# A state-space block and eight experts in one sweep over the batches: four batches in flight instead of three, and key sums formed as rows-by-features products

## The chip, the cores and the metric

The kernel runs on one core of a Trainium2 chip. The metric is device time in microseconds (us) of that core, as the median of three runs. TensorE (PE) multiplies matrices into PSUM, which has eight banks of 128x512 float32 here; VectorE (DVE), ScalarE (ACT) and GpSimd (POOL) work beside it, and SyncE (SP) issues most transfers. Each engine takes its instructions strictly in the order in which the program lists them. They meet through semaphores.

## The reference

Two layers of a modulated ("adaLN") network over x of 16 batches x 512 tokens x 128 features:

```
h = layernorm(x)*(1+ca)+sa
# layer 0, mixer: a selective state-space scan over the tokens, 256 channels, 16 states
xb, zb = split(h @ in_proj); xb = silu(conv4(xb)); zb = silu(zb)
dt, B, C = split(xb @ x_proj); dt = softplus(dt @ dt_proj + dt_bias)
for each of 16 states n:  s_n = exp(dt*A_n)*s_n(previous token) + dt*B_n*xb ;  y += C_n*s_n
x = x + ga * ((y + xb*D) * zb) @ out_proj
# layer 0, feed-forward: every expert computed, the best of 8 kept per token
h = layernorm(x)*(1+cb)+sb ;  x = x + gb * gate * (relu(h @ w1[e] + b1[e]) @ w2[e] + b2[e])
# layer 1, attention with random features (16 heads of 64), then ELU feed-forward and two norms
h3 = modulated layernorm(x)
k = h3@Wk ; v = h3@Wv ; kf = exp(k@proj - |k|^2/2 - M) + eps      # M: largest over ALL batches
kv = kf^T v ; ksum = sum over tokens of kf
out = (qf @ kv) / (qf @ ksum) @ Wo ...
# layer 1, feed-forward: 16 experts, two kept per token, plus a shared one
```

Since M is a maximum over all batches, the keys' sums of every batch must be formed before the queries of any batch can use them: the kernel has two sweeps.

## The kernel before, in words

**First sweep** (layer 0 and the key sums of layer 1). One step of the loop serves three batches: `a` runs its sixteen states, `b` (the one before) its experts and, in the same step, its keys, and `n` (the next) its norm, projections and convolution. A fourth name, `y`, only finishes key sums of the batch before `b`. 18 steps run: one with `n` alone, 16 with a state batch `a`, and one with `b` alone. Steps 3 to 14 are a hardware loop.

A step is cut by hand into slots. In each slot VectorE does for one state k, in this order: the input `u` (L1031), the scan `h` (L1038, `tensor_tensor_scan`), the weighing `zz` (L1047). Other work is listed between them. TensorE spreads B_k and C_k of each state over 128 partitions (`spread`, L801), which `u` and `zz` wait for. ScalarE makes the decay exponentials of the next state (`decay`, L591, two of them), which wait for the scan of this slot, since their buffer is double. GpSimd adds `zz` to the sum (L728).

Around this, in slots 2 to 11, lie the experts: 32 `ups` (each three 128x512 products in split precision, L174 to L176, by `split_product`), which go through a ring of three PSUM banks (2, 3, 4) that ScalarE's `relu` (L616) empties; eight `downs` (L854, 16 products of 128x128 each, banks 5 and 6), each taken by VectorE in the next slot (L1100). In slots 12 to 16 come the norm for layer 1 (L3), and eight key tiles (`key_tile`): each has three 128x512 products k, d, v (L869), a ScalarE square of k (L638) and a copy of v (L641), and on VectorE a reduction, a maximum and the exponent (L1125, L1128, L1131). At the end of the step: the largest key, softplus, the output projection (L809), the first residual, and the key exponentials (L648). The products `kf^T v` with a column of ones beside v (`key_sums`, L892) are 32 products of 128x129 in banks 5, 6 and 7. ScalarE copies them out (L655) and issues their store (L659).

The projections of `n` and `a` (x, z) and the logits share bank 7. Those of the step size dt and of B, C use banks 0 and 1.

**Second sweep.** Step by step, batch `n` loads its key sums, `c` computes queries, and `d` is in the feed-forwards. The C ring has two banks (0 and 1). At the end of a step the engines do this:

```
if n is not None:            # TensorE
    value_sums(n)            # two products, ring entries vs0, vs1
if d is not None:
    down(NX - 2, d); down(NX - 1, d)
...
if d is not None:            # VectorE
    dve.wait_ge(*mo(d, 1)); ... fo = ffn * gab
if n is not None:
    keys(n)                  # builds kvb for the next step's queries (L1821, L1823)
```

and the next step begins on TensorE with `query(0, "q")` (L174 to L176), which waits for its bank: the ring entry two before it must be done. Before, these entries were `vs0` and `vs1`, done when ScalarE had copied them (`evs_ok`, L1455).

## Time and profile before

| | us |
|---|---|
| median of three runs (range) | 3930.2 (3924.9 to 3931.4) |
| the profiled execution, its own time | 3920.3 |
| its span, first to last instruction | 3918.5 |
| PE busy / share | 3002.6 / 77% |
| DVE busy / share | 2898.4 / 74% |
| ACT busy / share | 1855.8 / 47% |
| POOL busy / share | 861.6 / 22% |
| mean granted TensorE clock, share of full | 0.889 |

The first sweep ends at about 2403 us, the second has its first VectorE work at 2421.7 us and takes the rest. A busy share is an average over both. A row of the timeline gives the start, how long it lasted (merged pieces with their count), engine, line, operation, output and input, and in brackets how long the engine had been idle and what released it. Tile names lose their numbers: `kvs` is `sq` for the key squares, `dt`, `dec`, `h`, `zz` are those above. A float32 product appears as two MATMUL records.

### The profile page before, as it was taken

The page shows a single profiled execution, that of the slowest core. Times are in us where ns is not written, and L with a number is a line of the kernel's source. Part 1 is how long each engine was busy: PE and PEld are TensorE (multiplying, and loading weights), DVE is VectorE, ACT ScalarE, POOL GpSimd, SP SyncE. Part 2 cuts the span into 40 slices and gives each one's busy share as a digit, 9 for nine tenths or more (in the row PEclk, how much of TensorE's full clock was granted, in tenths as well). Part 3 has the DMA queues.
Part 4 walks back from the last instruction along what each step waited for, and adds up shares of the span by engine and source line. Part 5 has one row for each costly group of instructions (what it writes and reads, how often), then busy time and mean ns, then how long its engine had stood idle before and what let it go on. Part 6 is the DMA issues. An engine that isn't in the chain of part 4 may idle for free. (4 is left out here: it accounts for less than half of the span.)

```text
span 3918.5 us, 51287 instructions
## 1 busy us (share of the span) xinstructions
PE 3002.6 (77%) x16104; PEld 2238.1 (57%) x16104; DVE 2898.4 (74%) x4942; ACT 1855.8 (47%) x2856; POOL 861.6 (22%) x590
## 2 busy tenths in 40 slices
PE   2478678777877867867877785788887888888886
PEld 1156446546545645645644663666666666666665
DVE  4888888888888888888888844666666666666664
ACT  3456546646645645645654642433333333333332
POOL 0433332333233323233323310011111111111111
PEclk6589889889988988988988897999999999999998
DMA  2000000000000000000000001000000000000000
GB/s 98 4 11 8 18 12 12 12 11 12 12 12 16 7 17 11 7 17 11 7 17 8 13 9 62 21 16 15 15 15 21 15 15 15 15 15 15 23 7 10
DMA packets 49767, 64.28 MB, mean 16 GB/s; under 512 B 3584, under 2 KB 36416, under 8 KB 49184
## 3 DMA queue, kind: packets, MB, share of 16 engines
q1 hardware_dynamic: 47392, 54.93, 4.3%
q10 hardware_dynamic: 2304, 8.46, 0.5%
q8 instruction: 37, 0.61, 0.1%
q14 instruction: 34, 0.28, 0.0%
HBM read 41.78 MB, written 21.60 MB: 16 GB/s over the span
## 5 line engine op out<-in xcount | busy, mean ns | idle before, releaser
L728 POOL TENSOR_TENSOR acc<-acc,zz 128x1024 f32<-128x1024 f32 x256 | 605.6, 2365 | 1400.4 <-DVE h L1038 1376.6
L1038 DVE TENSOR_TENSOR_SCAN h<-dec,u 128x1024 f32<-128x1024 f32 x256 | 584.4, 2283 | 3.5
L591 ACT ACTIVATE dec<-dt,aneg 128x512 f32<-128x512 f32 (+1 forms) x512 | 340.2, 712 | 439.1 <-DVE h L1038 415.2
L801 PE MATMUL bank<-S,pick_sb 96*128 96x512 bf16 x512 | 218.8, 439 | 386.1 <-DVE zz L1047 321.9
L854 PEld LDWEIGHTS bank<-one_sb,hid 128*128 128x128 f32 x4096 | 477.4, 192 | 4.6
L854 PE MATMUL bank<-one_sb,hid 128*128 128x128 f32 x4096 | 478.6, 274 | 0.0
L801 PEld LDWEIGHTS bank<-S,pick_sb 96*128 96x128 bf16 x512 | 52.6, 105 | 548.6 <-DVE zz L1047 375.7
L158 POOL TENSOR_SCALAR n_ve<-n_mv 128x4 f32<-128x4 f32 x96 | 33.5, 349 | 1344.3 <-DVE n_mv L141 1344.3
L1047 DVE TENSOR_TENSOR zz<-h,bank 128x1024 f32<-128x1024 f32 x256 | 312.5, 1221 | 8.8
L1031 DVE TENSOR_TENSOR u<-dtx,bank 128x1024 f32<-128x1024 f32 x256 | 311.0, 1215 | 9.9 <-DVE dtx L1024 7.4
L1446 ACT ACTIVATE uq<-uq 128x512 f32<-128x512 f32 x128 | 80.8, 631 | 359.9 <-DVE uq L1809 359.9
L616 ACT ACTIVATE hid<-banks,one_sb 128x512 f32<-128x512 f32 x336 | 227.5, 687 | 49.7 <-PE banks L176 48.1
L1508 ACT ACTIVATE th<-bank 128x512 f32<-128x512 f32 x160 | 95.6, 597 | 304.7 <-PE bank L176 303.7
L1100 DVE COPY_PREDICATED facc<-oh,bank 128x512 f32<-128x512 uint32 x128 | 93.0, 727 | 183.9 <-PE bank L854 183.5
L174 PE MATMUL bank<-h4h,low 128*128 128x512 f32 x192 | 102.2, 532 | 94.7 <-DVE sl L1893 69.9
L174 PE MATMUL banks<-hT2h,w_low 128*128 128x512 f32 x336 | 151.1, 450 | 21.3 <-ACT hid L616 21.3
L1711 PE MATMUL bank<-two_sb,hm 128*128 128x128 f32 x1280 | 158.9, 277 | 2.3 <-DVE hm L1899 2.3
L1711 PEld LDWEIGHTS bank<-two_sb,hm 128*128 128x128 f32 x1280 | 153.1, 193 | 10.6 <-issue 6.7
L1642 PEld LDWEIGHTS bank<-two_sb,aT 128*128 128x128 f32 x1024 | 142.0, 201 | 16.0 <-ACT aT L1467 4.0
L1626 PE MATMUL banks<-kvb,qT 128*128 128x130 f32 x1024 | 144.5, 286 | 5.6 <-DVE at L1835 5.6
L1899 DVE SCALAR_TENSOR_TENSOR hm<-sl,bank 128x512 f32<-128x512 f32 x160 | 109.9, 687 | 49.7 <-PE bank L1702 44.6
L1642 PE MATMUL bank<-two_sb,aT 128*128 128x128 f32 x1024 | 142.1, 284 | 3.0 <-ACT aT L1467 3.0
(256 smaller groups left out, 6897.5 us busy)
## 6 DMA issues: line engine op xcount, KB each, us to landing
kv_dram<-kvs ACTq DMA_DIRECT2D x16, 516.5 KB, 3.1
kvl<-kv_dram SPq DMA_DIRECT2D x16, 516.5 KB, 3.5
xs<-in_x SPq DMA_DIRECT2D x16, 256.0 KB, 2.8
x<-in_x SPq DMA_DIRECT2D x16, 256.0 KB, 2.8
x_dram<-x SPq DMA_DIRECT2D x16, 256.0 KB, 2.1
h_dram<-hT SPq DMA_DIRECT2D x16, 256.0 KB, 2.0
h<-h_dram SPq DMA_DIRECT2D x16, 256.0 KB, 2.6
x2s<-x_dram SPq DMA_DIRECT2D x16, 256.0 KB, 2.7
```

The source lines that it names most:

```text
L174: pe.matmul(dst, lhs[1], rhs[0], start=True, stop=False)
L591: act.activation(dec[:, k % 2, g, g:], dt[:, g, g:], ACT.Exp, scale=aneg[:, g, k:k + 1]).then_inc(dec_ok.sem, 1)
L616: act.activation(hid[:, e % 2, f, :], bank1(f"up{n}"), ACT.Relu, bias=b1c[:, n:n + 1]).then_inc(hid_ok.sem, 1)
L728: pool.tensor_tensor(acc[:, :, :], acc[:, :, :], zz[:, k % 2, :, :], ALU.add)\
L801: pe.matmul(banks[which][:, :], pick_sb[:, at:at + 1].to_broadcast([96, P]), S[0:96, :], start=True, stop=True).then_inc((cbc if which els ...
L854: last = pe.matmul(bank1(f"down{e}")[:, j * D:(j + 1) * D], hid[:, e % 2, f, j * P:(j + 1) * P], w2[:, e, f, :], start=(f == 0), stop=(f = ...
L1031: dve.tensor_tensor(u[:, :, :], dtx[:, :, :], mid(banks[0][:, :], G), ALU.mult)\
L1038: dve.tensor_tensor_scan(h[:, :, :].rearrange("p g t -> p (g t)"), dec[:, k % 2, :, :].rearrange("p g t -> p (g t)"), u[:, :, :].rearrange ...
L1047: dve.tensor_tensor(zz[:, k % 2, :, :], h[:, :, :], mid(banks[1][:, :], G), ALU.mult)\
L1626: last = pe.matmul(pair[:, k // 2, at_k:at_k + 2 * HW], qT[:, m % 2, k * P:(k + 1) * P], kvb[:, 4 * s + k, :], start=True, stop=True)
L1642: last = pe.matmul(banks[4][:, j * D:(j + 1) * D], aT[:, m % 2, k * P:(k + 1) * P], wo[:, 4 * s + k, :], start=False, stop=(s == 1 and k = ...
L1711: last = pe.matmul(banks[7][:, j * D:(j + 1) * D], hm[:, q, j * P:(j + 1) * P], w, start=(q == 0 and j == 0), stop=(q == NX - 1), skip_gro ...
```

## The change

**First sweep, four roles.** A step now serves `y` (two before the state batch: its norm L3 and its keys), `b` (one before: gated output, first residual, experts), `a` (states) and `n`. There are 19 steps: one with `n` alone, 16 with `a`, one with `b` and `y`, one with `y` alone. Slots run 0 to 16. All tables of slots are new, and a bank's next use now waits for the last use by a list of names and roles (`freed`, `free1`).

**Places.** z's projections go into the ring of three banks beside the ups; x, B/C/dt and logits have bank 7 to themselves, so banks 0 and 1 hold the spreads alone. ScalarE's `decay` stands first in its slot, before the relus. The positive part of dt moves from VectorE (`positive`, L1016, two of 128x512) to ScalarE (`magnitude`, one more activation each). B and C are split in a second tile `Sn` and copied to `S` by ScalarE (`keep_split`).

**Key sums.** No v and no copy of v. Instead h3 is turned back to rows (`back3`, `keep_rows`), and `products` forms h3^T kf as eight products of 128x512 (four for each half). `sums` forms the sums over tokens by eight 32x512 products with ones, four of them into the four quarters of one bank. `turn_sums` adds the quarters and turns them to columns by eight 128x128 products. In the second sweep `key_values` multiplies the loaded h3^T kf by Wv: eight products of 128x128 in two new ring entries kv0, kv1, which are free when VectorE's `keys` is done (`kvb_ok`).

```diff
-            UPS = {2: (0, 1), 3: (2, 3), 4: (4, 5), 5: (6, 7), 6: (8, 9), 7: (10, 11), 8: (12, 13), 9: (14, 15)}
-            DOWNS = {3: 0, 4: 1, 5: 2, 6: 3, 7: 4, 8: 5, 9: 6, 10: 7}
-            KEYS = {13: (0, 1), 14: (2, 3), 15: (4, 5), 16: (6, 7)}
-            GATE = {4: 0, 5: 1}
+            KEYS_PRE = {5: (5,), 6: (7,)}
+            KEYS_POST = {2: (0, 1), 3: (2, 3), 4: (4,), 5: (6,)}
+            TILE_A = {3: 1, 4: 2, 5: 4, 6: 6}
+            TILE_Z = {2: 0, 4: 3, 5: 5, 6: 7}
+            UPS_PRE = {4: (2,), 7: (8,), 8: (11, 12), 9: (16,), 10: (18,), 11: (20,), 12: (23,), 13: (25,),
+                       14: (27,), 15: (29,)}
+            UPS_POST = {3: (0, 1), 4: (3,), 5: (4, 5), 6: (6, 7), 7: (9, 10), 8: (13, 14, 15), 9: (17,), 10: (19,),
+                        11: (21, 22), 12: (24,), 13: (26,), 14: (28,), 15: (30, 31)}
+            DOWNS = {6: 0, 7: 1, 9: 2, 10: 3, 12: 4, 13: 5, 15: 6, 16: 7}
+            EXPS = {7: 0, 8: 1, 9: 2, 10: 3}
+            XIN = {9: 0, 10: 1}
+            CONV = {10: 0, 11: 1}
+            ring = ["oproj", "turn3", "k0", "back3", "turn2", "k1", "k2", "up0", "up1", "k3", "up2", "k4", "up3",
+                    "k5", "k6", "up4", "up5", "z0", "z1", "k7", "up6", "up7"]
...
+                    def step(s):
+                        y, b, a, n = roles(s)
+                        for slot in range(SLOTS):
                             if a is not None and slot + 1 <= NS - 1:
                                 decay(slot + 1, a)
...
+                            if a is not None and slot == 6:
+                                silu_z(0, a)
+                                silu_z(1, a)
...
+                            if y is not None:
+                                for m in KEYS_PRE.get(slot, ()):
+                                    key_square(m, y)
+                            if b is not None:
+                                for q in UPS_PRE.get(slot, ()):
+                                    relu(q, b)
...
+                        if n is not None:
+                            keep_split(a, n)
                             decay(0, n)
+                        if y is not None:
+                            store_sums(y)
...
-                    def key_sums(j, a, b, n):
+                    def products(half_k, y, s):
+                        pe.wait_ge(*h3n_ok(y, 1))
+                        free1(pe, f"g{half_k}", s)
+                        for j in range(J):
+                            pe.wait_ge(*kf(y, j + 1))
+                            last = pe.matmul(bank1(f"g{half_k}"), h3n[:, j, :], Ek[:, j, half_k * T:(half_k + 1) * T],
+                                             start=(j == 0), stop=(j == J - 1))
+                        last.then_inc(gps.sem, 1)
+
+                    def sums(half_k, y, s):
+                        free1(pe, f"ks{half_k}", s)
+                        for j in range(J):
+                            last = pe.matmul(bank1(f"ks{half_k}")[32 * j:32 * j + 32, :], ones[:, 0:32],
+                                             Ek[:, j, half_k * T:(half_k + 1) * T], start=True, stop=True)
+                        last.then_inc(ksps.sem, 1)
...
-        ringC = [("vs0", evs_ok, 1), ("vs1", evs_ok, 2)]
+        ringC = [("vs0", evs_ok, 1), ("vs1", evs_ok, 2), ("kv0", kvb_ok, 1), ("kv1", kvb_ok, 1)]
...
+                def key_values(c):
+                    pe.wait_ge(*kv_in(c, 16))
+                    for s in range(2):
+                        freeC(pe, f"kv{s}", c)
+                        for r in range(PR // 2):
+                            pr = s * (PR // 2) + r
+                            last = pe.matmul(bankC(f"kv{s}")[:, r * P:(r + 1) * P], kvl[:, pr * P:(pr + 1) * P],
+                                             wv[:, pr * P:(pr + 1) * P], start=True, stop=True)
+                        last.then_inc(kvps.sem, 1)
...
                     if n is not None:
                         value_sums(n)
+                        key_values(n)
                     if d is not None:
                         down(NX - 2, d)
```

ScalarE, first sweep, the looped step. Before, two gate activations (zs) lie in two slots, the relus (hid) between them, and the spare rows are the waits:

```order
L591 ACTIVATE dec<-dt,aneg 128x512
L591 ACTIVATE dec<-dt,aneg 128x511
L552 ISA
L554 ACT_TABLE_LOAD
L554 ACTIVATE zs<-bank 128x512
L614 REGISTER_ALU
L615 REGISTER_ALU
L616 ACTIVATE hid<-banks,one_sb 128x512
```

Now, in slot 6 (Gs is the tile of the key squares, here that of tile 7):

```order
L621 ACTIVATE dec<-dt,aneg 128x512
L621 ACTIVATE dec<-dt,aneg 128x511
L573 ISA
L575 ACT_TABLE_LOAD
L575 ACTIVATE zs<-bank 128x512
L573 REGISTER_ALU
L575 ACTIVATE zs<-banks 128x512
L671 REGISTER_ALU
L675 ACTIVATE Gs<-banks 128x512
```

The square of key tile 7 and the relus of ups 6 and 7 (the rows that follow) now stand behind the decays, a table load and both gates.

TensorE, first sweep, slot 15 to the end of the looped step as it is now (L921 is a down, L966 the new sums, L869 the spreads, L976 the turn of the sums):

```order
L921 MATMUL bank<-one_sb,hid 128x128 x16
L497 REGISTER_ALU
L966 MATMUL bank<-Ek,ones 32x512 x4
L869 MATMUL bank<-S,pick_sb 128x512
L917 REGISTER_ALU
L497 REGISTER_ALU
L921 MATMUL bank<-one_sb,hid 128x128 x16
L966 MATMUL bank<-Ek,ones 32x512 x4
L865 REGISTER_ALU
L869 MATMUL bank<-S,pick_sb 128x512 x2
L976 MATMUL bank<-thirty,kss 128x128 x8
```

Before, this place held the largest key, the output projection, the spreads and half of the key sums; the downs were over by slot 10. Now two downs and the sums stand in it, and the last spread of C is behind the first sums.

TensorE, second sweep, the border of the looped step. Before:

```order
L1601 MATMUL bank<-keep_sb,hsB 128x512 x2
L1711 MATMUL bank<-two_sb,hm 128x128 x4
L1709 REGISTER_ALU
L1711 MATMUL bank<-two_sb,hm 128x128 x4
L1381 REGISTER_ALU
L1381 COMPARE_AND_BRANCH
```

Now:

```order
L1686 MATMUL bank<-keep_sb,hsB 128x512 x2
L1691 ISA
L1432 ISA
L1696 MATMUL bank<-keep_sb,kvl 128x128 x4
L1432 REGISTER_ALU
L1696 MATMUL bank<-keep_sb,kvl 128x128 x4
L1807 MATMUL bank<-two_sb,hm 128x128 x4
L1805 REGISTER_ALU
L1807 MATMUL bank<-two_sb,hm 128x128 x4
L1466 REGISTER_ALU
L1466 COMPARE_AND_BRANCH
```

Eight products came in ahead of the last two downs (L1807), and the query products that open the next step follow the branch as before.

## Rows read from the trace of the kernel before

**Rows 1.** Busy time in one looped step of the first sweep (windows)
```profile
core 0: us, PE busy (x) PEld busy (x) DVE busy (x) ACT busy (x) POOL busy (x), PEclk, DMA share, GB/s
1026.80:1169.76 142.96, 111.22 (x554) 78.24 (x553) 120.42 (x161) 80.14 (x116) 43.74 (x25) 0.88 0.04 12
```

**Rows 2.** Line L1024, once at the end of each step (source view)
```profile
L1024 DVE TENSOR_TENSOR dtx<-dt,xc x16: 1224/1225/1226, 78.8 to 2166.1; 128x1024 f32<-128x1024 f32 x16
```

**Rows 3.** VectorE's waits in the step of rows 1: total, times, longest
```profile
DVE facc L1100 <- PE bank L854: 9.2, 5, 2.4
...
DVE ssq L1125 <- ACT kvs L638: 2.5, 2, 1.9
...
DVE xh L149 <- POOL n_rs L160: 1.5, 1, 1.5
...
DVE idx L1079 <- DVE m L1075: 0.2, 1, 0.2
```

**Rows 4.** VectorE's timeline, first sweep
```profile
177.95 1.23 DVE L1024 TENSOR_TENSOR dtx<-dt,xc 128x1024 f32<-128x1024 f32 x1
...
1117.06 2.29 DVE L1038 TENSOR_TENSOR_SCAN h<-dec,u 128x1024 f32<-128x1024 f32 x1
...
1121.86 2.29 DVE L1038 TENSOR_TENSOR_SCAN h<-dec,u 128x1024 f32<-128x1024 f32 x1
...
1141.40 0.68 DVE L1125 TENSOR_REDUCE ssq<-kvs 128x8 f32<-128x512 f32 x1
...
1143.32 2.28 DVE L1038 TENSOR_TENSOR_SCAN h<-dec,u 128x1024 f32<-128x1024 f32 x1
...
1161.74 1.40 DVE L1016 TENSOR_SCALAR dt<-bank,one_sb 128x512 f32<-128x512 f32 x2
```

**Rows 5.** ScalarE's timeline, first sweep
```profile
1061.82 0.69 ACT L616 ACTIVATE hid<-bank,one_sb 128x512 f32<-128x512 f32 x1
...
1112.21 1.33 ACT L591 ACTIVATE dec<-dt,aneg 128x512 f32<-128x512 f32 x2 [8.04 <-DVE h L1038]
1113.56 1.28 ACT L549 ACT_TABLE_LOAD   x1
...
1137.74 0.58 ACT L638 ACTIVATE kvs<-bank 128x512 f32<-128x512 f32 x1
...
1163.79 4.27 ACT L648 ACTIVATE Ek<-Ek,ncb 128x1024 f32<-128x1024 f32 x4
```

**Rows 6.** TensorE's timeline, first sweep
```profile
1054.88 3.73 PE L854 MATMUL bank<-one_sb,hid 128*128 128x128 f32 x32
...
1060.22 0.40 PE L174 MATMUL banks<-hT2h,w_low 128*128 128x512 f32 x1
...
1062.32 0.39 PE L801 MATMUL bank<-S,pick_sb 96*128 96x512 bf16 x1
...
1113.49 0.61 PE L801 MATMUL bank<-S,pick_sb 96*128 96x512 bf16 x1 [7.85 <-DVE zz L1047]
...
1141.77 1.02 PE L869 MATMUL bank<-one_sb,hT 128*128 128x512 f32 x2
```

**Rows 7.** VectorE at a border between steps of the second sweep (timeline)
```profile
2939.30 0.69 DVE L1952 TENSOR_TENSOR fo<-bank,gab 128x512 f32<-128x512 f32 x1 [1.25 <-PE bank L1711]
...
2942.78 0.69 DVE L1803 TENSOR_REDUCE qs<-qsqb 128x8 f32<-128x512 f32 x1
```

**Rows 8.** TensorE at the same border (timeline)
```profile
2935.44 1.91 PE L1601 MATMUL bank<-keep_sb,hsB 128*128 128x512 f32 x4
2937.18 2.08 PE L1711 MATMUL bank<-two_sb,hm 128*128 128x128 f32 x16
2939.02 0.48 PE L174 MATMUL bank<-high,h3l 128*128 128x512 f32 x1
```

**Rows 9.** The end of the first sweep: last take, and the last store's issue (timeline)
```profile
2358.28 0.72 DVE L1100 COPY_PREDICATED facc<-oh,bank 128x512 f32<-128x512 uint32 x1 [2.84 <-PE bank L854]
...
2402.99 0.34 ACTq L659 DMA_DIRECT2D kv_dram<-kvs  x1
```

More of the change, by code:

```diff
@@ new lines, in adaln_depth2 @@
+            DOWNS = {6: 0, 7: 1, 9: 2, 10: 3, 12: 4, 13: 5, 15: 6, 16: 7}
+            TAKES = {slot + 1: e for slot, e in DOWNS.items() if slot + 1 < SLOTS}
+            EXPS = {7: 0, 8: 1, 9: 2, 10: 3}
[3 more added lines that the diff above has]
+                    "k5", "k6", "up4", "up5", "z0", "z1", "k7", "up6", "up7"]
+            ring += [f"up{n}" for n in range(8, 25)] + ["gates", "up25", "up26", "b2"]
@@ new lines, in roles, with free1 @@
+            def roles(s):
+                return tuple(batch_at(s, off) for off in (YES, BEF, NOW, NXT))
+            def free1(pe, name, s):
+                names = uses[bank_of[name]]
+                at = names.index(name)
+                before = [(back, other) for back in range(3) for other in reversed(names[:at] if back == 0 else names)]
+                for back, other in before:
+                    off, done, count = freed[other]
+                    batch = batch_at(s, off - back)
+                    if batch is not None:
+                        pe.wait_ge(*done(batch, count))
+                        return
@@ L899, in step @@
-                    def step(a, b, n, y):
-                        for slot in range(END):
+                    def products(half_k, y, s):
[6 more added lines that the diff above has]
+                        last.then_inc(gps.sem, 1)
@@ L901, in step @@
+                    def step(s):
+                        y, b, a, n = roles(s)
+                        for slot in range(SLOTS):
                             k = slot - 1
```

828 lines of the change are left out of this document (427 added, 401 removed).

## The prediction, made before the changed kernel had run

> **What bounds the kernel now.** I read the page first, then windows of one step of each sweep, VectorE's waits in one step, and the timelines of single slots. One looped step of the first sweep takes 143 us; VectorE is busy for 120.4 of them, TensorE for 111.2, at a granted clock of 0.88 [rows 1]. From the first to the last L1024, once a step, are 2087.3 us; less the first interval of 99.2 there are fourteen of 142.0 [rows 2, 4]. So VectorE sets the step, and what can be saved is its idle time: twelve lines of waits, from 9.2 down to 0.2 us, sum to 20.4 us [rows 3]. Of these 9.2 are takes that wait for a down: ups and down of an expert are packed into each slot there. VectorE's own work with its gaps is then 143.0 - 20.4 = 122.6 us. A better order of the other engines can win at most the waits for them, some 19 us a step, and only if it makes no new ones.
>
> **The change, part by part.** *Removed from VectorE*: the positive part of dt, 1.4 us [rows 4]. With 0.7 us of short waits between its own instructions, which stay, its work is 122.6 - 1.4 + 0.7 = 121.9 us a step. A bare slot (scan to scan) is 4.8 us, a key tile 1.9 [rows 4].
>
> *TensorE's work* hardly changes. Gone are eight v products and 32 narrow ones. A 512-wide float32 product keeps it for 0.86 us (two records, 1.02 with the tail of the last); a down for 3.6; an up for 0.70 (2.10 us from the record at 1060.22 to the spread, nine records) [rows 6]. Eight v products were 6.9 us and the 32 narrow ones about 8. New are eight h3^T kf products, 6.9, the turn back, 0.6, the turn of the sums, 1.9, and the sums. For these no row is near: no product here fills a quarter of a bank. Bounds: four after one another 4 x 0.86 = 3.4 us, four at once 0.9. I take the middle, 2.1 for each half. TensorE's sum per step stays near 102 us.
>
> The Trainium skill, page "TensorE: Matmul & The Clock Gate", section "Part 3: Packing small matmuls", says that products whose outputs lie in different 32-partition strips run concurrently; no run here shows it yet. By it the sums would be near the 0.9 us; that is a rival below.
>
> *ScalarE* loses eight v copies (0.6 each), three sum copies and two of eight table loads, and gains two relus of dt, five copies and one more small one: about even, 80 us of 142 [rows 1]. But its place changes. In every slot it now first waits for that slot's scan, then makes two decays (1.3 us), and only then the relus (0.7) and squares (0.6) [rows 5] that TensorE's three-bank ring waits for. So each slot holds a loop: scan, decays, relus, ups, down, take. I walked through the slots with the rows' durations; S is the end of the slot's scan. VectorE's new waits:
> - slots 1 and 2: both norms wait for GpSimd, as before at 1.5 for one [rows 3]: 0.5 + 1.5. Key tile 0 waits for its square at S + 1.9 while zz ends at S + 1.2: 0.8.
> - slot 5, tile 5: the same, 0.8.
> - slot 6, tile 7: decays 1.3, table load 1.3, two gates 1.1, square 0.6: S + 4.3 against S + 1.2: **3.0**.
> - slot 7: ups 6 and 7 wait for the banks of z (S + 3.2), down 0 ends at S + 8.3, the largest key is spread at S + 9.0 to 10.5 (after six idle us TensorE is slow: 7.85 us of idling are followed by a spread of 0.61 instead of 0.39 [rows 6]). VectorE is there at S + 7.5: **2.2**.
> - slot 10: up 14 waits for the relu of up 11, S + 2.0; four ups, turn, spreads, down 2: S + 9.5. The bare slot 9 is over, so the take waits **2.6**, the convolution for x another 1.0; slot 11 1.4.
> - slot 13: decays, three relus, a copy, two table loads (one before, one after) and the silu, two relus, two copies end 11.3 after the scan of slot 11; VectorE is there at 8.7: **2.6**; slot 14 0.6.
> - slots 14 to 16 on TensorE: 1.3 to the bias product's end, 5.1 ups, products, dt, then 2.5 of ups, down, sums, down: take 6 waits 1.2, the last C 0.3, softplus 1.8 (its logarithm stands behind the copy of the first sums).
>
> Sum 20.3, so a step is 121.9 + 20.3 = **142.2 us**: the takes' waits are gone, but waits on ScalarE have come in their place.
>
> *Transfers and GpSimd.* SP now loads the residual x and both gate rows for `b` when x2 of the batch before is done, at a step's end. VectorE wants them after gated output, norm, scan, zz and projection, about 8 us later, and such loads land in 2.8 us (the page's list of transfers): nothing. The stores are the same size. GpSimd's L2 norm now stands before its first addition and L3's after its last; the additions have a slot of 7 us for 2.4 us of work, so only the two norm waits listed remain. The copy of B and C at the step's end waits for the last sums and ends before VectorE's second residual (3.1 us): hidden, but 1 to 2 us late if the sums take 3.4.
>
> *The sweep.* Start and first interval stay (78.8 + 99.2). The next step has no keys: 142.2 less eight tiles (15.4), one norm and the largest key (2) and their waits (5), 120. Then thirteen steps of 142.2. The last L1024 comes at 2146.6 instead of 2166.1: -19.5. From there to the end of the last take were 2359.0 - 2166.1 = 192.9 [rows 2, 9]. Now follow a step without n, 127 (142 less about 15 for n), and one for b and y that TensorE sets: eight downs 28.6, 32 ups 22.4, sixteen key products 13.8, h3^T kf 6.9, sums 2.1, rest 6, and 15 of opening chain, 95. That is 222: +29. The last batch's keys now stand alone, without v (-4 of the 44 us from the last take to the store's issue [rows 9]), but behind its exponentials (4.3 us for four [rows 5]) stand, instead of narrow products that ran along with them, four products (3.4), both sums (4.2), the turn (1.9) and copies: +7. The first sweep so ends 12 to 14 us later.
>
> *The border of the second sweep.* Before, value sums, two downs, then at once the first query (2939.02) [rows 8]; fo and the keys' assembly ran beside it until 2942.78, where the first reduction found its square ready [rows 7]. Now eight 128-wide products (16 records at 0.117, by the down of 3.73 for 32 [rows 6]) delay the last downs by 1.8 us, and the first query waits for `kvb_ok`, so for fo and the assembly; then come three records (0.9 with the tail) and the square (0.6) before the reduction. 1.8 + 1.5 = 3.3 us, 15 times: **+50**. The assembly itself, four half-size instructions for two, is even. Nothing covers it: every engine's next step starts from this border. If slack covered it, it would cost nothing.
>
> Sum: -19.5 + 29 + 3 + 50 = about **+64**. The profiled execution took 3920.3 us: 3984; it lay 10 us under the median of 3930, so I forecast **3990** for a median.
>
> **The rivals.**
> - *ScalarE's order hides after all*, 0.20. For: it is busy for only 80 of 143 us, and some waits of my list may overlap. Then slots 6, 7, 10 and 13 lose half of their 10 us: step near 137, 15 steps x 5.2 = -78: **3912**. It decides on the other side where the step falls under 138.2, since 15 x 4 = 60 pays for the rest.
> - *The sums at once*, 0.15: four quarter-bank products in the time of one, as the section named above has it. The sums then end 1.2 us earlier in each half: softplus waits 0.9, the last C nothing, so a step is 141.0 and the end 2 us shorter: **3970**. In the other direction, at 3.4 us each, 4010, which is in my forecast's own range.
> - *The second sweep's border is covered*, 0.08: the later query shortens waits that follow within the step: **3940**. Against: VectorE is in line from fo to the reduction without a gap [rows 7].
> - *The loop gets slower*, 0.17. TensorE's idle pieces of 3.5 to 6 us in slots 1, 5, 6 and 8 leave it at the lower level (1.2 GHz) while ups and downs are due, 2 to 3 us in two places: step 147, **4062**. Against: before, it idled as long (7.85 us [rows 6]) and met its takes.
> - The forecast itself, 0.40, its own range 3955 to 4030.
>
> **How the numbers follow.** A difference of 0.2% (8 us) is about what a measurement of this kernel can tell from none. Slower: 0.40 + 0.15 + 0.17 + 0.05 of the covered border = 0.77. Faster: 0.17 of the first rival and 0.01 = 0.18. The rest, 0.05, is within. The range 3900 to 4060 leaves out some 0.08 of the fast rival and 0.09 of the slow one.
>
> **What will show it.** In the new profile: L1024's successor thirteen times at 142 us apart; VectorE's wait for ScalarE's square of 3 us in slot 6 and for the copy of B and C of 2.6 in slot 13, while waits of takes for downs fall from 9.2 to about 4; the clock near 0.88; at the second sweep's border a TensorE idle of 3.5 us before the first query, released by VectorE's kvb, and 95.7 us a step for 92.4. If the distance of steps is under 138 us, my reading of ScalarE's order is wrong; if the border shows no such idle, the ring is.

## The result, and the profile after

The changed kernel takes 4122.3 us (median of 4 runs, 4116.4 to 4127.1) against 3927.5 for the kernel before in the same comparison (also 4 runs): ratio 1.049, 95% interval [1.047, 1.051]. The forecast was 3990. The sign is right, the size is not: +195 us instead of +64. The profiled executions differ by 199.8 us of span (4118.3 and 3918.5), divided by a few landmarks of the two timelines:

| stretch | before | after | difference | forecast |
|---|---|---|---|---|
| start to the last dtx (L1024, now L1097) | 2166.1 | 2249.6 | +83.5 | -19.5 |
| from there to the end of the last take | 192.9 | 222.8 | +29.9 | +29 |
| to the last store's issue | 44.0 | 48.0 | +4.0 | +3 |
| to the first VectorE work of sweep two | 18.7 | 18.4 | -0.3 | 0 |
| sweep two up to the first fo (two borders) | 151.7 | 160.2 | +8.5 | |
| its next 14 steps, fo to fo | 1276.0 | 1349.2 | +73.2 | +50 with the row above |
| the last step and the end | 69.1 | 70.1 | +1.0 | |

The end of the first sweep came out within 2 us. The looped step and the border of the second sweep did not. Busy time in a looped step, as [rows 1]:

```profile
core 0: us, PE busy (x) PEld busy (x) DVE busy (x) ACT busy (x) POOL busy (x), PEclk, DMA share, GB/s
1047.94:1198.31 150.37, 110.92 (x525) 75.23 (x525) 122.58 (x159) 73.42 (x113) 44.67 (x25) 0.89 0.04 12
```

150.4 us, not 142.2. VectorE is busy for 122.6 us although 1.4 us of work left it: [rows 1] had 120.4. Line L1097, as [rows 2]:

```profile
L1097 DVE TENSOR_TENSOR dtx<-dt,xc x16: 1225/3254/3261, 84.2 to 2249.6; 128x1024 f32<-128x1024 f32 x16
```

The same instruction took 1.22 us sixteen times before; now only the first does, and the median is 3.25. VectorE's waits in the step from 897.84 to 1047.94, as [rows 3]:

```profile
DVE facc L1177 <- PE bank L921: 5.6, 3, 3.2
DVE ssq L1203 <- ACT Gs L675: 4.3, 3, 3.0
DVE u L1103 <- issue: 4.0, 2, 3.7
DVE cb L1222 <- PE bank L949: 3.2, 1, 3.2
DVE cv L1066 <- ACT xpad L564: 3.0, 2, 1.9
DVE Sn L1079 <- ACT Sn L583: 2.1, 1, 2.1
DVE zz L1119 <- PE bank L869: 0.8, 1, 0.8
DVE dt L1094 <- ACT cv L608: 0.7, 1, 0.7
```

The walk through the slots is nearly all there: 3.0 for the square in slot 6, 3.2 (forecast 2.2) for the largest key, takes, copies of x, the split (2.1 for 2.6); the takes fell from 9.2 to 5.6. Not there are the waits of the two norms for GpSimd (2.0 forecast), and a wait of 0.8 at zz was not forecast. All waits, with the short ones that are not shown, sum to 25.4 us; 3.7 of them are the one line that was not forecast at all, "issue": a wait for nothing that the profile shows. Another 1.6 are short waits between VectorE's own instructions, for which the forecast had 0.7. What is left, 20.1 us, stands against the forecast's 20.3. Where the wait for issue is, VectorE's timeline over a border of steps shows:

```profile
1044.40 1.22 DVE L1119 TENSOR_TENSOR zz<-h,bank 128x1024 f32<-128x1024 f32 x1
1046.35 1.56 DVE L1094 TENSOR_TENSOR dt<-xpad,cv 128x1024 f32<-128x1024 f32 x1 [0.73 <-ACT cv L608]
1047.94 3.25 DVE L1097 TENSOR_TENSOR dtx<-dt,xc 128x1024 f32<-128x1024 f32 x1
...
1055.96 0.38 DVE L141 BATCH_NORM_AGGREGATE n_mv<-n_st 128x2 f32<-128x6 f32 x4 [0.16 <-DVE n_st L136]
1059.83 1.22 DVE L1103 TENSOR_TENSOR u<-dtx,bank 128x1024 f32<-128x1024 f32 x1 [3.50 <-issue]
```

GpSimd at the same time:

```profile
1044.45 5.67 POOL L794 TENSOR_TENSOR acc<-acc,zz 128x1024 f32<-128x1024 f32 x2 [4.65 <-DVE h L1110]
```

The loop's branch stands between n_mv and u. The wait of 3.4 to 4.1 us is there at the end of each of the loop's twelve turns but the first. The two full steps without it take 147.1 and 147.0 us, the others 150.0 to 150.4. The border of the second sweep, VectorE, as [rows 7]:

```profile
3181.32 0.69 DVE L2055 TENSOR_TENSOR fo<-bank,gab 128x512 f32<-128x512 f32 x1 [3.00 <-PE bank L1807]
3181.93 1.46 DVE L1918 TENSOR_SCALAR kvb<-kvl,sfac 64x8 f32<-64x8 f32 x2
3183.40 1.98 DVE L1926 SCALAR_TENSOR_TENSOR kvb<-bank,sfac,evs 64x256 f32<-64x256 f32 x4
3187.12 0.69 DVE L1900 TENSOR_REDUCE qs<-qsqb 128x8 f32<-128x512 f32 x1 [1.75 <-ACT qsqb L1527]
```

and TensorE, as [rows 8]:

```profile
3179.33 1.95 PE L1807 MATMUL bank<-two_sb,hm 128*128 128x128 f32 x16
3185.52 0.47 PE L174 MATMUL bank<-high,h3l 128*128 128x512 f32 x1 [4.24 <-DVE kvb L1926]
```

The idle time before the first query is there, released by kvb, 4.2 us for 3.5. From fo to the first reduction are now 5.8 us in this step and 6.5 in most others (before 3.5 [rows 7]), and 14 steps average 96.4 us for 91.1.

### The profile page after: what moved, and what is told of

It reads as the page before. It is cut to its first block and busy times, and to the rows that moved or that the text cites. A ratio compares the mean times of both kernels' runs of the same rounds, so it can differ in the third digit from the quotient of the medians.

```text
span 4118.3 us, 51446 instructions
## 1 busy us (share of the span) xinstructions
PE 3078.8 (75%) x15912; PEld 2234.9 (54%) x15912; DVE 2946.7 (72%) x4942; ACT 1752.8 (43%) x2792; POOL 872.4 (21%) x590
## 5 line engine op out<-in xcount | busy, mean ns | idle before, releaser
L794 POOL TENSOR_TENSOR acc<-acc,zz 128x1024 f32<-128x1024 f32 x256 | 618.4, 2416 | 1200.9 <-DVE h L1110 1193.1
L869 PE MATMUL bank<-S,pick_sb 96*128 96x512 bf16 x512 | 227.3, 449 | 379.4 <-DVE u L1103 224.2
L921 PEld LDWEIGHTS bank<-one_sb,hid 128*128 128x128 f32 x4096 | 498.8, 199 | 14.7 <-issue 2.2
L921 PE MATMUL bank<-one_sb,hid 128*128 128x128 f32 x4096 | 496.7, 281 | 0.9 <-DVE facc L1177 0.8
L158 POOL TENSOR_SCALAR n_ve<-n_mv 128x4 f32<-128x4 f32 x96 | 49.5, 516 | 1677.0 <-DVE n_mv L141 1677.0
L869 PEld LDWEIGHTS bank<-S,pick_sb 96*128 96x128 bf16 x512 | 53.3, 104 | 589.8 <-DVE u L1103 270.6
L174 PE MATMUL banks<-hT2h,w_low 128*128 128x512 f32 x336 | 210.3, 626 | 95.7 <-ACT hid L653 64.4
L943 PE MATMUL bank<-pk,hT 128*128 128x512 f32 x256 | 157.8, 703 | 9.4 <-DVE Ek L1210 7.9
L1900 DVE TENSOR_REDUCE qs<-qsqb 128x8 f32<-128x512 f32 x128 | 87.3, 682 | 102.9 <-ACT qsqb L1527 102.8
L1807 PE MATMUL bank<-two_sb,hm 128*128 128x128 f32 x1280 | 157.3, 276 | 2.3 <-DVE hm L2002 2.3
L174 PE MATMUL bank<-hT2h,w_low 128*128 128x512 f32 x176 | 100.1, 569 | 74.5 <-ACT zs L575 74.5
L174 PEld LDWEIGHTS banks<-hT2h,w_low 128*128 128x128 f32 x336 | 72.6, 216 | 149.6 <-ACT hid L653 85.9
L1807 PEld LDWEIGHTS bank<-two_sb,hm 128*128 128x128 f32 x1280 | 151.0, 193 | 3.3 <-DVE hm L2002 2.7
```

Of the source, the lines that this page charges most:

```text
L174: pe.matmul(dst, lhs[1], rhs[0], start=True, stop=False)
L794: pool.tensor_tensor(acc[:, :, :], acc[:, :, :], zz[:, k % 2, :, :], ALU.add)\
L869: pe.matmul(banks[which][:, :], pick_sb[:, at:at + 1].to_broadcast([96, P]), S[0:96, :], start=True, stop=True).then_inc((cbc if which els ...
L921: last = pe.matmul(bank1(f"down{e}")[:, j * D:(j + 1) * D], hid[:, e % 2, f, j * P:(j + 1) * P], w2[:, e, f, :], start=(f == 0), stop=(f = ...
L943: pe.matmul(bank1(f"{name}{m}"), hT3[:, j * P:(j + 1) * P], w[:, half_m * T:(half_m + 1) * T], start=True, stop=True).then_inc(done.sem, 1)
L1807: last = pe.matmul(banks[7][:, j * D:(j + 1) * D], hm[:, q, j * P:(j + 1) * P], w, start=(q == 0 and j == 0), stop=(q == NX - 1), skip_gro ...
```

## Experiments

Each ran beside the kernel before on its own chip; its median there was 3925 to 3929. Medians, and ratios to the kernel before:

| run | edit | us | ratio, 95% interval |
|---|---|---|---|
| e1 | changed, 50 idle instructions before the loop | 4094.4 | 1.042 [1.038, 1.045] |
| e2 | before, 79 idle instructions | 3949.5 | 1.005 [1.004, 1.007] |
| e3 | changed, keys ahead of fo | 4061.0 | 1.034 [1.030, 1.037] |
| e4 | changed, own banks for h3^T kf Wv | 4089.3 | 1.040 [1.036, 1.043] |
| e5 | changed, dt behind the residual | 4123.8 | 1.050 [1.048, 1.053] |
| e6 | changed, square 7 first | 4139.0 | 1.054 [1.051, 1.056] |
| e7 | e1, e3 and e5 together | 4024.9 | 1.024 [1.022, 1.027] |
| e8 | before, keys ahead of fo | 3922.2 | 0.998 [0.997, 0.9995] |
| e9 | changed, last addition cut (result incomplete) | 4096.3 | 1.043 [1.040, 1.046] |
| e10 | e7, down 0 later | 4028.1 | 1.026 [1.023, 1.029] |
| e11 | changed, sums in turn | 4166.2 | 1.059 [1.057, 1.061] |
| e12 | e7, gates ahead of the decays | 3933.7 | 1.001 [1.000, 1.002] |
| e14 | changed, gates ahead of the decays | 4043.0 | 1.029 [1.027, 1.031] |
| e13 | e12, convolution later | 3899.3 | 0.993 [0.991, 0.994] |
| e15 | e13, take 2 later | 3878.6 | 0.987 [0.985, 0.989] |

**The wait at the branch (e1, e2).** In the changed kernel's step five packets of 8 KB of instructions are fetched, at 907.9, 910.7, 920.5, 972.7 and 1034.9 us. The branch itself is at 906.0. From the program's order the last three fetches fall at instructions 32, 160 and 288 of VectorE's loop body of 333, so 128 apart (in the trace's records of VectorE, some of which are extra, at 38, 170 and 293 of 337). Its loop starts 49 instructions earlier than before and, if blocks are 128 long, lies over four of them.

```diff
                     dve.wait_ge(a_exp, 1)
+                    for _ in range(100):        # e1; e2, on the kernel before: range(158)
+                        dve.wait_ge(a_exp, 1)
```

> The changed kernel with 50 idle wait instructions (100 waits on a count reached long before, two to an instruction) ahead of the first sweep's loop on VectorE, nothing else. Fetch theory: the wait of 3.5 us before the first state input after the loop's branch is VectorE's loop body lying over four blocks of 128 instructions (the trace fetches 5 packets of 8 KB a step, at loop positions near 32, 160 and 288 of 333), with the branch's target thrown out by the last fetch. Shifted by 50 the body lies in three: instruction packets fall from 89 to about 34, the eleven waits of 3.4 to 4.1 us vanish, each looped step takes 147.1 us as the two unrolled ones do, not 150.2: 34 us less, about 4088. Rival: the wait belongs to what stands there (the semaphores, GpSimd, the end of the norm), then all stays within 8 us of 4122 and the row still shows 3.5 us.

> The kernel before with 79 idle wait instructions ahead of VectorE's first loop. Fetch theory: its body (314 instructions) begins 49 later than that of the changed kernel, so 79 more put it in the same position to the blocks of 128 and it now lies over four of them: instruction packets rise from 34 to about 90, a wait of 3 to 4 us with nothing that releases it appears at the branch of each of the last eleven looped steps (there was a wait of 0.6 there), 11 x 3 = +33 us, about 3960. Rival (position has no part in it): within 8 us of 3928.

The page's line of instruction packets, of the changed kernel, e1 and e2 (packets, MB, share):

```profile
q14 instruction: 89, 0.73, 0.1%
```

```profile
q14 instruction: 34, 0.28, 0.0%
```

```profile
q14 instruction: 90, 0.74, 0.1%
```

e1 has no wait for issue at the branch any more, and its looped steps take 146.6 to 147.0 us; e2 has eleven of 3.1 to 3.2 us, one of them this:

```profile
1042.30 1.22 DVE L1033 TENSOR_TENSOR u<-dtx,bank 128x1024 f32<-128x1024 f32 x1 [3.06 <-issue]
```

So the wait is made and taken away by instructions that do nothing: it hangs on the position of VectorE's loop body to the blocks in which instructions are fetched. The median gains 28 us here; the steps alone say 37 (11 x 3.4). In the kernel before e2 lost 22 us, less than the 33 expected. Only some 11 of them lie in the looped steps, which grew by 1.0 us (143.4 for 142.4): the wait for the logits fell there from 2.2 to 0.7 us and the wait of 0.6 behind dtx went. Another 7 lie at the start, where the first dtx comes at 86.1 us for 78.8, which fits an estimate of 0.09 us for each idle instruction (e1 starts some 4 us later, too).

In e1's profile the last dtx comes 36 us earlier, but the span is only 20 shorter: its second sweep was slower (97.4 us a step for 96.4), with no edit there. So a difference of 1 us a step of the second sweep between two profiles shows nothing.

The Trainium skill, page "Runtime: NRT & Kernel Launch", section "Instruction fetch mechanics", says that each engine has a small instruction memory refilled in blocks, and that a taken branch to a target outside the window forces a fetch before execution goes on. By that rule the prediction would have had to look at the branch. The trace agrees with it at the branch, but its fetches are of 8 KB, 128 instructions apart, where the page has blocks of 16 KiB.

**GpSimd's last additions (e5, e9).** e5 moves dt and dtx behind the last take and the second residual.

```diff
-                        norm_stats(dve, L3, x2, b, passed)      # the end of second_residual
...
-                        if n is not None:
-                            softplus(n)
                         if b is not None:
                             take(E0 - 1, b)
                             second_residual(b)
+                        if n is not None:
+                            softplus(n)
+                        if b is not None:
+                            norm_stats(dve, L3, x2, b, passed)
```

> The changed kernel with VectorE's last take and second residual (up to the sum x2) ahead of dt and dtx at the step's end, and the norm's statistics behind them; GpSimd's last two additions are then over before dt begins. Theory (the two additions on GpSimd slow VectorE's instructions whose operands all lie in SBUF): dtx takes 1.2 us, not 3.25, dt 1.2, not 1.56, GpSimd's additions 2.4 each and not 5.7 for both, and the wait of 0.7 for dt's logarithm is covered: 2.4 to 3.1 us a step, 35 to 45 us less, 4077 to 4087. Rival (they are long for another reason, such as ScalarE reading dt): they keep 3.25 and 1.56, and at most the 0.7 is won, 10 us.

```profile
1043.88 3.11 DVE L1185 SCALAR_TENSOR_TENSOR facc<-facc,erec,b2s 128x128 f32<-128x128 f32 x4
...
1048.63 1.23 DVE L1094 TENSOR_TENSOR dt<-xpad,cv 128x1024 f32<-128x1024 f32 x1 [0.20 <-DVE x L1195]
1049.89 1.22 DVE L1097 TENSOR_TENSOR dtx<-dt,xc 128x1024 f32<-128x1024 f32 x1
```

Half of it came true: dt and dtx are short again. But the time did not move, since the first four instructions of the residual, which also have all their inputs in SBUF, now stand beside the additions and take 3.11 us for 1.14, and the last take waits 0.7 us for its down. The price goes to whoever stands there. e9 takes the addition away:

```diff
-                        pool.tensor_tensor(acc[:, :, :], acc[:, :, :], zz[:, k % 2, :, :], ALU.add)
+                        n_t = T if k < NS - 1 else 8
+                        pool.tensor_tensor(acc[:, :, :n_t], acc[:, :, :n_t], zz[:, k % 2, :, :n_t], ALU.add)
```

> The changed kernel, but GpSimd's last addition of each batch (the sixteenth state) adds only the first 8 tokens of each group: this leaves out nearly all of the last state's part of y. Theory (the additions slow VectorE's instructions that read only SBUF, and in the late-softplus kernel the price only moved from dtx to the second residual): with GpSimd idle after some 1047 us of the profile's step, dtx takes 1.2 instead of 3.25 us and the step falls by 2.0 to 2.4 us in each of 15 steps: 30 to 36 us less, 4086 to 4092. Rival (what follows waits for something else, the branch's instruction fetch or the decays, so that nothing comes through): within 8 us of 4122.

dtx takes 1.2 us, steps 148.1 to 148.9: 26 us less, just short of the expected 30 to 36. In the changed kernel's rows the two engines take turns: GpSimd's pair ends at 1050.12, and dtx, begun at 1047.94, ends 1.07 us later, just short of its own 1.22. Before, GpSimd's last pair was over at 1159.29, ahead of the gated product, which needs its sum, and so ahead of dt and dtx:

```profile
1154.45 4.84 POOL L728 TENSOR_TENSOR acc<-acc,zz 128x1024 f32<-128x1024 f32 x2 [6.42 <-DVE h L1038]
```

The Trainium skill, page "SBUF — State Buffer", section "SBUF: two separate sides", has this as an exclusive lock between a GpSimd instruction that reads SBUF and a VectorE instruction with two SBUF inputs, held for the whole instruction; the trace agrees, and u and zz, which read one input from PSUM, keep their 1.2 us beside additions.

**The second sweep's border (e3, e4, e8).**

```diff
+                    if n is not None:           # e3; the same on the kernel before: e8
+                        keys(n)
                     if d is not None:
                         dve.wait_ge(*mo(d, 1))
...
-                    if n is not None:
-                        keys(n)
```

> The changed kernel with VectorE's assembly of the keys (3.4 us) ahead of fo at the border of the second sweep, in its 3.0 us wait for the last down. Ring theory: the first query waits for that assembly, so TensorE's idle time of 4.2 us at the border shrinks to 1 us or less, fo comes 0.5 to 1 us later, and the step falls from 96.4 by 2.5 to 3.5 us: 37 to 50 us less, 4072 to 4085. Rival (the eight products before the last downs are what costs, and the later query is covered within the step): under 15 us.

```diff
-        ringC = [("vs0", evs_ok, 1), ("vs1", evs_ok, 2), ("kv0", kvb_ok, 1), ("kv1", kvb_ok, 1)]   # e4
+        ringC = [("vs0", evs_ok, 1), ("vs1", evs_ok, 2)]
...
                     pe.wait_ge(*kv_in(c, 16))
+                    pe.wait_ge(*at_ok(c, 0))
                     for s in range(2):
-                        freeC(pe, f"kv{s}", c)
...
-                            last = pe.matmul(bankC(f"kv{s}")[:, r * P:(r + 1) * P], kvl[:, pr * P:(pr + 1) * P],
+                            last = pe.matmul(banks[2 + s][:, r * P:(r + 1) * P], kvl[:, pr * P:(pr + 1) * P],
```

> The changed kernel with the eight products of the loaded h3^T kf in banks 2 and 3 (free once the last quotient of the batch before is taken) and not in the ring of banks 0 and 1, so that the first query no longer waits for VectorE's assembly; products, downs and assembly stay in their order. Ring theory: of the 5.2 us a step that the border costs, 1.8 are the products ahead of the downs and stay; the query starts right behind the last down and the rest, 2.3 to 3.4 us a step, goes: 35 to 50 us less, 4072 to 4087. Rival (the assembly of 3.4 us on VectorE sets the first reduction anyway, since it stood there before too): under 10 us less.

> The kernel before with VectorE's assembly of the keys ahead of fo at the border of its second sweep. Theory (the border is on the path in both kernels): the assembly uses the wait of 1.25 us and no longer runs beside GpSimd's addition, fo comes 0.6 us later, the first reduction 1.5 to 2.1 us earlier: 21 to 30 us less, 3897 to 3906. Rival (covered within the step, or fo's delay takes it back): within 8 us of 3927.

VectorE's border in e3:

```profile
3153.64 0.48 DVE L1918 TENSOR_SCALAR kvb<-kvl,sfac 64x8 f32<-64x8 f32 x2
3154.14 1.98 DVE L1926 SCALAR_TENSOR_TENSOR kvb<-bank,sfac,evs 64x256 f32<-64x256 f32 x4
3156.68 0.69 DVE L2057 TENSOR_TENSOR fo<-bank,gab 128x512 f32<-128x512 f32 x1 [0.56 <-PE bank L1807]
3158.01 0.69 DVE L1900 TENSOR_REDUCE qs<-qsqb 128x8 f32<-128x512 f32 x1 [0.64 <-ACT qsqb L1527]
```

e3 wins 61 us, more than expected: its 14 steps average 91.7 us, 4.7 less, and only 0.6 over the kernel before, though the eight products still stand ahead of the downs. So the order of VectorE's work is nearly all of the cost; 0.6 us a step would be left for the products, which is less than the 1.0 by which two profiles differ with no edit there. e4 wins 33 us, just under its range (its four runs lie between 4079 and 4104). TensorE no longer idles at the border, but the assembly of 3.4 us still stands ahead of the first reduction, and TensorE idles later instead:

```profile
3180.35 0.80 PE L174 MATMUL bank<-pq_high,h3l 128*128 128x512 f32 x1 [4.01 <-DVE uq L1906]
```

The wait in the ring and the assembly ahead of the reduction lie in parallel, and only e3 takes both away. In the kernel before the same edit wins next to nothing (3 us, where 21 to 30 were expected): from fo to the second exponent it is 2.7 us shorter, but its later waits for squares and quotients are longer. Why it is all given back there was not settled.

**Slots 6 and 7 (e6, e10, e14, e12).** What stands there in the changed kernel, on ScalarE:

```profile
960.10 1.33 ACT L621 ACTIVATE dec<-dt,aneg 128x512 f32<-128x512 f32 x2 [5.58 <-DVE h L1110]
961.45 1.28 ACT L575 ACT_TABLE_LOAD   x1
...
963.72 0.61 ACT L675 ACTIVATE Gs<-banks 128x512 f32<-128x512 f32 x1
```

and on TensorE, which goes on without a gap from the first of these rows to the second down:

```profile
963.40 0.50 PE L174 MATMUL bank<-hT2h,w_low 128*128 128x512 f32 x1 [4.04 <-ACT zs L575]
...
965.18 5.06 PE L921 MATMUL bank<-one_sb,hid 128*128 128x128 f32 x32
...
970.29 0.39 PE L949 MATMUL bank<-keep_sb,bmx 128*128 128x128 f32 x2
```

e6 puts the line `for m in KEYS_PRE.get(slot, ()): key_square(m, y)` ahead of both `silu_z`.

> The changed kernel with the square of key tile 7 ahead of both gates of z on ScalarE in slot 6. The wait for it falls from 3.0 to some 0.6 us. Theory A (the wait is a price of ScalarE's order, as the prediction had it): the step is 2.4 us shorter, 14 steps, 34 us less, 4088. Theory B (TensorE's chain behind it, ups 6 and 7, down 0 and only then the largest key, sets slots 6 and 7 together): the wait for the largest key grows from 3.2 by the same 2.4, and the time stays within 8 us of 4122.

The square's wait fell to 0.63 us and the largest key's rose to between 6.0 and 7.1 us (3.2 to 3.8 before this edit); the gates came 0.6 us later, and 17 us were lost. Theory A is refuted. Of theory B the wait moved as it says, but the time left its 8 us, as the chain now starts later.

e10 moves `downs(0, b, s)` behind `largest(y, s)` in slot 7 and `take(0, b)` to the slot's end.

> The kernel with three edits (4025), and in it down 0 moved on TensorE from the end of slot 6 to behind the largest key's spread in slot 7, its take to the end of slot 7. The wait for the largest key (3.2 us) is then the time of TensorE's queue ahead of it: theory (down 0, 3.6 to 5 us, stands between the ups and the largest key and sets it): the wait falls under 0.5 us, the take then waits some 0 to 1 us, the step falls by 2 to 3 us from 146.8: 28 to 42 us less, 3983 to 3997. Rival (the ups 6 and 7 behind both gates set it, or down 1, which now waits for the take of down 0 in the same bank, loses it again in slot 8): within 10 us of 4025.

The rival holds. The wait for the largest key is gone and take 1 waits 3.1 us instead; the step is 146.8 as in e7. The chain is TensorE's, and its wait shows wherever VectorE meets it first. It begins at the gates. e14 moves these, alone, and e12 in the kernel of e7:

```diff
+                            if a is not None and slot == 6:
+                                silu_z(0, a)
+                                silu_z(1, a)
                             if a is not None and slot + 1 <= NS - 1:
                                 decay(slot + 1, a)
...
-                            if a is not None and slot == 6:
-                                silu_z(0, a)
-                                silu_z(1, a)
```

> The changed kernel with the gates' order alone: both gates of z ahead of the decays on ScalarE in slot 6. In the kernel with three edits this took 91 us, 5.7 a step, and removed the waits of 3.9 us for the largest key and 2.4 for the square. If this cause is independent of the others, 85 to 95 us less than 4122 here too, 4027 to 4037, with a step of 144 to 145 us for 150.2. Rival (part of it came only together with the later softplus or the missing fetch): 50 us or less, over 4070.

> The kernel with three edits (4025), and in it both gates of z ahead of the decays on ScalarE in slot 6; ScalarE idles for 5.6 us there before the decays, and z's products end 4.6 us before them. Theory (slots 6 to 8 are one chain on TensorE: gates, ups 6 and 7, down 0, largest key, down 1; it starts at the gates): TensorE's idle time of 5.7 us before up 6 falls under 1 us, the wait for the square of tile 7 from 3.0 to about 0.6, the chain is 3 to 4 us earlier, the step 143 to 144 us instead of 146.8: 38 to 55 us less, 3970 to 3987. Rival (the wait goes to the relus of ups 6 and 7, which still stand behind the decays, and the chain stays): the wait for the largest key grows by what the square's wait loses, within 10 us of 4025.

79 us less alone, where 85 to 95 were expected, and 91 in company, where 38 to 55 were: the largest of all effects, and the chain was underrated. In e12 gates and table loads lie in ScalarE's idle time, down 0 begins behind the ups without a wait, and the largest key's spread now waits for VectorE:

```profile
919.98 3.73 PE L921 MATMUL bank<-one_sb,hid 128*128 128x128 f32 x32
...
925.18 0.47 PE L949 MATMUL bank<-keep_sb,bmx 128*128 128x128 f32 x2 [1.25 <-DVE bmx L1217]
```

A part of the price is TensorE's clock. In the changed kernel TensorE idles 4.0 us ahead of up 6, and down 0 takes 4.6 to 5.1 us in every looped step, at a granted clock of 0.73 in the step shown; in the kernel before every down of those steps takes 3.7 to 3.8. In e12 TensorE does not idle there, and down 0 takes 3.7 to 3.8 us in eight of twelve looped steps. The two stretches, changed kernel and e12, in the columns of the table of busy times above:

```profile
965.18:970.24 5.06, 5.06 (x34) 5.05 (x33) 2.35 (x4) 1.97 (x2) 0.00 (x0) 0.73 0.00 0
919.98:923.71 3.73, 3.73 (x34) 3.56 (x32) 3.07 (x4) 2.53 (x5) 2.37 (x1) 1.00 0.00 0
```

By these durations, as an estimate, about 1 us of the 5.6 a step is clock. The rest is work that starts earlier.

**Together, and beyond (e7, e13, e15).**

> The changed kernel with three edits together: 50 idle instructions ahead of VectorE's first loop (28 us alone), the keys ahead of fo in the second sweep (61 alone), and dt behind the second residual (35 to 45 alone). If the three causes are independent they add: 4122 - 28 - 61 - 40 = 3993, from 3985 to 4000. If one covers another, less. What is left over 3927 is then the loop's waits on ScalarE and TensorE and the longer end of the first sweep.

97 us less, outside the expected range, which had counted 40 for e5: e1 and e3 alone make 89, and e5 adds little, as by itself.

> The kernel with four edits (3934: idle instructions, keys first, late softplus, gates first), and in it the convolution of the first half of the channels behind slot 10's weighing and not ahead of its scan. VectorE waits there 1.9 us for ScalarE's copy of x, and 1.0 for the second half's in slot 11. Theory (VectorE sets the step, these waits are on its path): both go, 2 to 3 us a step, 15 steps, 30 to 45 us less, 3889 to 3904. Rival (TensorE's chain of downs sets slots 9 to 12, and its takes wait longer by as much): within 8 us of 3934.

> As the kernel with the later convolution, and the take of down 2 also behind slot 10's weighing. Down 2 is waited for 2.9 us ahead of slot 10's scan. Theory (VectorE sets the step): 1 to 3 us a step less again, 15 to 45 us under the kernel with the later convolution. Rival (down 3 uses the same bank and waits for this take, which comes 3.5 us later, so the wait goes to slot 11): within 8 us of it or slower.

```diff
-                            if b is not None and slot in TAKES:
+                            if b is not None and slot in TAKES and slot != 10:      # e15
...
-                                if slot in CONV:
-                                    convolve(CONV[slot], n)
+                                if slot == 11:      # e13 and e15
+                                    convolve(1, n)
...
+                            if b is not None and slot == 10:      # e15
+                                take(TAKES[slot], b)
+                            if n is not None and slot == 10:      # e13 and e15
+                                convolve(0, n)
```

Both times lie in the expected ranges: 34 and 21 us less, steps of 138.0 and 136.6 us (141.2 in e12). In e13 no wait took the place of those removed. In e15 a part came back: the waits at zz for the spreads of C grew from 1.0 to 3.3 us a step, the second of them in slot 10 itself, where the spread stands behind down 2 on TensorE, so the step fell by 1.5 us and not by 2.9.

```profile
935.37 1.22 DVE L1121 TENSOR_TENSOR zz<-h,bank 128x1024 f32<-128x1024 f32 x1 [1.77 <-PE bank L869]
```

Unlike the wait for the largest key, these waits mostly vanish when VectorE comes later. e15 is the best version, 1.3% faster than the kernel before.

**The sums (e11).**

```diff
-                            last = pe.matmul(bank1(f"ks{half_k}")[32 * j:32 * j + 32, :], ones[:, 0:32],
-                                             Ek[:, j, half_k * T:(half_k + 1) * T], start=True, stop=True)
+                            last = pe.matmul(bank1(f"ks{half_k}"), ones[:, :],
+                                             Ek[:, j, half_k * T:(half_k + 1) * T], start=(j == 0), stop=(j == J - 1))
```

> The changed kernel with the sums over tokens formed by four products one behind the other into a whole bank (each row the sum over all tokens, and 1/128 in place of 1/32 in the turn), not into the four quarters of a bank. The trace of the changed kernel has eight records of a half's sums in 1.06 us. If the quarters ran at once, each half now takes 3.4 to 3.6 us, the last spread of C and the copy behind the second half come 2.4 us later each, and VectorE's wait at zz or at dt grows by 1 to 3 us a step: 15 to 45 us more, 4137 to 4167. Rival (a narrow product is just short, four of 32 columns in turn, and nothing waits for it): within 8 us of 4122.

A half's sums take 3.60 us in turn and 1.06 in quarters:

```profile
1048.72 3.60 PE L966 MATMUL bank<-Ek,ones 128*128 128x512 f32 x8
```

```profile
1041.20 1.06 PE L966 MATMUL bank<-Ek,ones 128*32 128x512 f32 x8
```

(first e11, then the changed kernel.) In the changed kernel's single records the four quarters of a group start within 0.02 us of each other and last 0.6 each, so they do run at once and are not just short; in e11 one starts every 0.43 us. This agrees with the rule that the prediction weighed (the Trainium skill, page "TensorE: Matmul & The Clock Gate", section "Part 3: Packing small matmuls").

The step grows by 3.3 us and the time by 44, but not by the sums' length alone. The wait for dt's logarithm grows from 0.7 to 2.5 us and that for the largest key to 4.4, while dtx, which now begins after GpSimd's additions, takes 1.23 us again. And the wait at the branch is 5.4 us in each turn and not 3.4 to 4.1:

```profile
1069.78 1.22 DVE L1103 TENSOR_TENSOR u<-dtx,bank 128x1024 f32<-128x1024 f32 x1 [5.38 <-issue]
```

Why the branch costs more here was not settled, and what the quarters are worth in a kernel without this wait was not run.

## Why the prediction was wrong

By the table above some 103 us of the miss lie in the first sweep up to its last dtx (+83.5 for -19.5) and 32 in the second sweep.

- **The slots' external waits: right.** Where and on whom VectorE waits was forecast nearly place by place, and their sum is 20.1 us for 20.3. The largest key was 1.0 us dearer (up to 1.6 in other steps), the last softplus 1.1 cheaper, the norms' 2.0 did not come (in e1, without the wait at the branch, 0.5 of it shows). That the sum fits so well is partly luck. The rival "ScalarE's order hides after all" fell.
- **The failed step: "its work is 121.9 us a step"**, taken from durations before. By it VectorE is busy for 119.0 us (120.4 less 1.4); it is busy for 122.6. The same instructions take longer beside GpSimd: dtx +2.0, dt +0.4, the gates' product gp +0.7 (0.90 us, 0.19 before), xh +0.3. That is 3.4 us a step, some 50 us, of which e9 returned 26 by cutting one addition; the other pieces were read from the trace and not tested by themselves. Before, the gated product waited for the last addition, so neither dt nor dtx stood beside one.
- **A cost left out: the loop's branch.** Priced at nothing, it costs 3.4 us in eleven steps, 28 us by e1. It hangs on where the loop's body lies and not on what the step does: 50 idle instructions ahead of the loop take it away.
- Together: 3.6 us of busy time, 3.7 at the branch and 0.9 more of short waits, less 0.2 of the external ones, are 8.0, and the step shown missed by 7.9 (150.1 for 142.2).
- **The rival "the loop gets slower"** has the right side and a part of the mechanism. Behind an idle piece of 4.0 us in slot 6 down 0 runs at a mean granted clock of 0.73 (4.6 to 5.1 us for 3.7, some 1.1 us a step), and behind another of 4.0 us, ahead of the ups at 984.2 us, the clock is 0.71 up to 990.0. But its price was put at 4.8 us a step; most of the 8 us by which a step missed are the two costs above.
- **The sums: taken at 2.1 us, measured 1.06.** The rival "the sums at once" was right in its mechanism; it was hidden under the two costs above.
- **The second sweep's border: right mechanism, wrong size**, 5.2 us a step for 3.3, and the rival "covered" fell. (The step before is 91.1 us in the mean, not 92.4.) The split "1.8 + 1.5" was wrong too: e3, which changes the order alone, takes back 4.7 of the 5.2. Behind the wait TensorE, having idled 4.2 us, starts slow: its query records take 0.63 us, 0.40 before. The assembly was called even and takes 3.4 us for 3.0; it runs beside GpSimd's sum ob in both kernels (L1918 takes 1.46 us there, and 0.48 in e3, where it does not).
- **The ends: right.** +29.9 and +4.0 us for +29 and +3.
- **A slip of addition**: -19.5 + 29 + 3 + 50 is 62.5 and not 64. Nothing hangs on it.
- **What the prediction had as one wait of 3.0 us** (slot 6) was the head of a chain: gates, ups 6 and 7, down 0, largest key, down 1. The forecast of both waits was nearly right, but their cause was one, and moving two lines on ScalarE returns 79 to 91 us.

## What to carry to other kernels

A walk through the slots with durations from the trace found most waits within a microsecond here; it doesn't find what the durations themselves depend on. Look at what runs on GpSimd beside each instruction with both inputs in SBUF, and in loops at the page's count of instruction packets: if it grows with the steps, shift the body by idle instructions. Of two waits in adjacent slots, ask first whether one chain makes both; remove its head, not the wait that shows.

## What the hardware showed that was not expected

- VectorE's loop body of 333 instructions is fetched anew at each turn (5 packets of 8 KB) and pays 3.4 to 4.1 us at the branch (5.4 in e11) in one position; 50 instructions further it pays nothing. The body of 314 in the kernel before, moved by 79, pays 3.1 to 3.2, but its step grows by only 1.0 us. Four blocks of 128 instructions instead of three explain where the wait stands, but not its size; the block length is worked out from the places of three fetches.
- One 128x1024 addition on GpSimd (2.4 us) can delay a VectorE instruction with both inputs in SBUF by about 2 us, even one of 128x128 (2.38 us at most for 0.34 in L1185). Instructions with one input in PSUM keep their time.
- Four float32 products of 32x512 into four quarters of a bank take 1.06 us, and four of 128x512 in turn 3.60.
